# Two-layer vision kernel: the first layer's inverse Fourier product in 64x64 quarters of the array, with accumulators split by parity of the 8x8 block

## What is computed

```python
h = jnp.einsum('oi,bihw->bohw', w_in, x)          # 64 -> 3 x 170 channels
gate, x_sp, x_fr = jnp.split(h, 3, axis=1)
sp = conv_general_dilated(x_sp, w_dw, ... 3x3, feature_group_count=170)
xp = x_fr.reshape(b, 170, H // 8, 8, W // 8, 8).transpose(0, 1, 2, 4, 3, 5)
f = jnp.fft.rfft2(xp) * fft_weight                # over each block of 8x8 pixels
fr = jnp.fft.irfft2(f, s=(8, 8)) ...              # back in place
fused = gelu(gate) * (sp + fr)
return einsum('oi,bihw->bohw', w_out, fused)      # 170 -> 64 channels
```

## Time and profile before

| what | value |
|---|---|
| median of 3 runs | 10511.98 us (10511.55 to 10516.97) |
| the profiled execution: its time, and its span | 10515.79 us, 10514.0 us |
| TensorE clock granted, mean | 0.967 |
| PE busy, share of the span | 9748.7 us, 93% |
| DVE busy | 8528.3 us, 81% |
| ACT busy | 5724.7 us, 54% |
| chain that ended last, PE's share | 81% |

### The profile page before, as it was taken

One profiled execution on the slowest core, in us unless ns is written; L12 is line 12 of the kernel. 1 busy time (PEld: TensorE's weight loads), 2 busy tenths in 40 slices (PEclk: granted clock), 3 DMA queues, 4 the chain that ended last, 5 costly groups with the idle time before them and its releaser, 6 DMA issues.

```text
span 10514.0 us, 163193 instructions
## 1 busy us (share of the span) xinstructions
PE 9748.7 (93%) x60966; PEld 7369.1 (70%) x60966; DVE 8528.3 (81%) x12871; ACT 5724.7 (54%) x9047; POOL 1769.1 (17%) x1824
## 2 busy tenths in 40 slices
PE   1999988999999998998999999899899999989998
PEld 1777765757777775675777777576677777757666
DVE  7788878978788887888878888787886888788787
ACT  0555544656655554454765555455575555445557
POOL 0000003333300001233320000223331000033333
PEclk9999999999999999999999999899999999999999
DMA  4667665475676766446567676635566666564655
GB/s 119 141 139 143 139 144 193 163 225 147 153 147 140 144 140 177 167 169 212 156 149 144 140 143 136 207 142 194 176 172 129 127 128 127 121 210 160 213 155 150
DMA packets 1332286, 1650.52 MB, mean 157 GB/s; under 512 B 843676, under 2 KB 1076524, under 8 KB 1246124
## 3 DMA queue, kind: packets, MB, share of 16 engines
q1 hardware_dynamic: 1331500, 1640.09, 60.7%
HBM read 786.71 MB, written 515.00 MB: 124 GB/s over the span
## 4 chain that ended last, share of the span: by engine, by line
PE 81%; DVE 10%; issue 3%; ACT 3%; DMA 1%; POOL 1%; SPq 1%; DVEq 0%; POOLq 0%; ACTq 0%
PE ps L819 14%; PE ps L1733 12%; PE ps L1746 7%; PE ps L789 6%; PE ps L849 4%; PE ps L1311 4%; PE ps L780 4%; PE ps L833 4%; PE ps L1760 3%; DVE S L1515 3%; PE ps L1304 3%; PE ps L1383 2%; PE ps L873 2%; PE ps L860 2%; PE ps L795 2%
## 5 line engine op out<-in xcount | busy, mean ns | idle before, releaser
L1131 DVE SCALAR_TENSOR_TENSOR F<-U,LW,F 106x512 f32<-106x512 f32 x2048 | 1535.3, 750 | 54.4
L1733 PE MATMUL ps<-fp,Dwr 128*128 128x512 f32 x6144 | 1471.4, 389 | 0.0
L1733 PEld LDWEIGHTS ps<-fp,Dwr 128*128 128x128 f32 x6144 | 1153.3, 188 | 239.5
L1109 DVE TENSOR_TENSOR Z<-ps,LW 128x340 f32<-128x340 f32 x1024 | 522.7, 510 | 822.1 <-PE ps L789 821.1
L943 ACT ACTIVATE XF<-ps 128x340 f32<-128x340 f32 x1024 | 464.5, 454 | 1116.0 <-PE ps L780 1116.0
L819 PE MATMUL ps<-P,WP 128*128 128x512 f32 x3072 | 904.8, 416 | 32.3 <-DMA H<-P 32.3
L1311 PEld LDWEIGHTS ps<-RS,Bc 128*128 128x128 f32 x4096 | 555.0, 200 | 529.3 <-DVE RS L1300 302.3
L819 PE MATMUL ps<-H,WP 128*128 128x512 f32 x3072 | 918.3, 421 | 0.0
L1383 PE MATMUL ps<-fp,Bwr 128*128 128x512 f32 x3072 | 879.4, 426 | 21.3 <-DVE fp L1484 21.3
L1746 PE MATMUL ps<-XP,Cwr 128*128 128x512 f32 x3072 | 824.9, 405 | 75.0 <-DVE XP L1870 75.0
L1311 PE MATMUL ps<-RS,Bc 128*128 128x128 f32 x4096 | 677.1, 295 | 180.8 <-DVE RS L1300 180.8
(11 more groups left out here) (295 smaller groups left out, 20505.0 us busy)
## 6 DMA issues: line engine op xcount, KB each, us to landing
H<-P SPq DMA_DIRECT2D x512, 585.0 KB, 7.2
raw<-x SPq DMA_DIRECT2D x240, 640.0 KB, 11.5
fx_d<-fx SPq DMA_DIRECT2D x112, 1024.0 KB, 3.9
fl_d<-fp SPq DMA_DIRECT2D x112, 1024.0 KB, 5.5
fp<-fl_d SPq DMA_DIRECT2D x112, 1024.0 KB, 5.8
fx<-fx_d SPq DMA_DIRECT2D x112, 1024.0 KB, 5.4
x1h_d<-xo SPq DMA_DIRECT2D x256, 256.0 KB, 9.0
x1v_d<-xo SPq DMA_DIRECT2D x512, 128.0 KB, 7.8
```

The lines of the kernel that those rows point to most:

```text
L1109: e.tensor_tensor(Z[t % 2][:, 2 * c:2 * c + 2, :].rearrange("p a b -> p (a b)"), ps[6][:, 0:2 * HID], Wt, ALU.mult).then_inc(sem["z"], 1)
L1131: ins = e.scalar_tensor_tensor(o, u, wd[0:106, i:i + 1], o, ALU.mult, ALU.add)
L1733: ins = e.matmul(bank(m)[:], Dwr[:, w, c:c + 128], fq[n % 2][x][:, s2, :], start=(s2 == 0 and w == 0 and x == 0), stop=False)
```

## The change

`finv` is called once a tile and makes 32 products in place of 8. Each takes 64 frequencies (the half `hf` = block parity i) and 64 channels (the half q) of a group k, and a new 64x64 constant `Rblk` without zeros, kept beside Rinv in one tile Rall of 192 columns. The four products of a group thus lie in four different quarters of the array, and the two frequency halves write to different banks: the even blocks of the tile to ps2, the odd ones to ps3. So that the convolution and the gate of the same pixels are in the same bank, `conv` and `gate` no longer read 64 neighbouring columns for i, but 8 of every 16 columns (`px8`, and another view of xb). G and the banks are in that order too; `fu` puts the result back in pixel order in F128.

The order changes with it. On TensorE, chunk 0 of `xs` comes where the first `finv` was, and the whole inverse product is ahead of chunk 1 of `xs`. On VectorE both `fu` come after `z` of chunk 0 and three taps.

```diff
-    k["k_Rinv"] = Rb
+    k["k_Rinv"] = np.concatenate([Rb, np.tile(R, (2, 1))], 1)
...
-    Rinv, Rfwd = at("Rinv", [128, 128]), at("Rfwd", [128, 128])
+    Rall, Rfwd = at("Rall", [128, 192]), at("Rfwd", [128, 128])
+    Rinv, Rblk = Rall[:, 0:128], Rall[:, 128:192]
...
-            m = xb[t % 2][:, 512 * i:512 * i + 512].rearrange("p (k r w) -> p r k w", k=4, r=8)
+            m = xb[t % 2][:].rearrange("p (k r b w) -> p b r k w", k=8, r=8, b=2)[:, i]
...
-            col = 64 * i
+
+            def px8(v, r, c):
+                return v[:, r:r + 8, c:c + 128].rearrange("p r (k b w) -> p b r k w", k=8, b=2)[:, i]
+
...
-                    m = (u[:, 0:8, col:col + 64], u[:, 2:10, col + 1:col + 65], v[:, 0:8, col + 2:col + 66],
-                         v[:, 1:9, col:col + 64])[j]
+                    m = (px8(u, 0, 0), px8(u, 2, 1), px8(v, 0, 2), px8(v, 1, 0))[j]
...
-        def finv(t, i):
-            o = ps[2 + i][:].rearrange("p (r c) -> p r c", r=8)
-            for j in range(4):
-                if j % 2 == 0:
-                    e.wait_ge(sem["z"], 4 * (NT * b + t) + 2 * i + j // 2 + 1)
-                ins = e.matmul(o[:, :, 16 * j:16 * j + 16], Z[t % 2][:, 4 * i + j, 0:128], Rinv[:], start=False, stop=(j == 3))
-            ins.then_inc(sem["fi"], 1)
+        def finv(t):
+            for k in range(8):
+                if k % 2 == 0:
+                    e.wait_ge(sem["z"], 4 * (NT * b + t) + k // 2 + 1)
+                for i in range(2):
+                    hf = slice(64 * i, 64 * i + 64)
+                    o = ps[2 + i][:].rearrange("p (r k c) -> p r k c", r=8, k=8)[:, :, k, :]
+                    for q in (slice(0, 64), slice(64, 128)):
+                        ins = e.matmul(o[q], Z[t % 2][hf, k, q], Rblk[hf, :], start=False, stop=(k == 7))
+                    if k == 7:
+                        ins.then_inc(sem["fi"], 1)
...
-            m = F128[s][:].rearrange("c i (a q w) -> c q a i w", q=2, w=64)
+            m = F128[s][:].rearrange("c (a q w) -> c q a w", q=2, w=128)
...
-            finv(t, 0)
             xs(t + 1, 0)
...
                 conv(t, 1, range(3, 5))
+            finv(t)
             xs(t + 1, 1)
-            finv(t, 1)
...
-            e.tensor_tensor(F128[t % 2][:, i, :], ps[2 + i][:], G[t % 2][:, i, :], ALU.mult).then_inc(sem["fu"], 1)
+            o = F128[t % 2][:].rearrange("c (n b w) -> c b n w", b=2, w=8)[:, i]
+            u, v = [x.rearrange("c (n w) -> c n w", w=8) for x in (ps[2 + i][:], G[t % 2][:, i, :])]
+            e.tensor_tensor(o, u, v, ALU.mult).then_inc(sem["fu"], 1)
...
-            fu(t, 0)
             z(t + 1, 0)
             depthwise(t, range(4, 7))
+            fu(t, 0)
             fu(t, 1)
```

More of the change, by code:

```diff
@@ L224, in build @@
     G42 = [at(f"G42{i}", [106, 512]) for i in range(2)]
-    F128 = [at(f"F128{i}", [128, 2, 512]) for i in range(2)]
+    F128 = [at(f"F128{i}", [128, 1024]) for i in range(2)]
     F42 = [at(f"F42{i}", [106, 512]) for i in range(2)]
@@ L718, in ahead_0 @@
         e.dma_start(Rfwd[:], a["k_Rfwd"]).then_inc(sem["rt"], 16)
-        e.dma_start(Rinv[:], a["k_Rinv"]).then_inc(sem["rt"], 16)
+        e.dma_start(Rall[:], a["k_Rinv"]).then_inc(sem["rt"], 16)
     def l0_sp(e, b):
@@ L855, in finv42 @@
                 e.wait_ge(sem["ad"], NT * b + t)
-            R = Rinv[:].rearrange("k (a p c) -> k p a c", a=4, p=2)
+            R = Rinv.rearrange("k (a p c) -> k p a c", a=4, p=2)
             for k in range(8):
```

## The result

The change makes the kernel slower: 10759.5 us (median of 4 runs, 10755.7 to 10764.0) against 10514.5 us for the kernel before beside it (4 runs, 10511.6 to 10517.1). The ratio is 1.0234, with a 95% interval of 1.0221 to 1.0247. That is 245 us, or 0.96 us for each of the 256 tiles. The profiled execution has a span of 10755.5 us. The forecast was 10673 us, 161 us or 0.63 us a tile.

What follows compares the result with a forecast made beforehand. TensorE's queue was taken as the bound. Terms of -0.52, +1.08, +0.05 and +0.02 made +0.63 us a tile, over 256 tiles +161 us on 10512: 10673 us, range 10395 to 10870.

Steps and rivals of the forecast that it cites:

- slower case: Whole kernel: short runs cost as in the sum or some way from it, 10545 to 10870 us, chance 0.46.
- product: Inverse product on TensorE: quarters run four at a time, 1.22 us against 1.74, gaining 0.52 us a tile.
- reads of P and H: Convolution records on TensorE: 56 added runs at 0.8 ns, 45 ns on 24 records, losing 1.08 us a tile.
- reads of xb: Gate and block 4 records on TensorE: runs stay aligned, costing nothing to 0.03 us, 0.02 in the sum.
- `fs` behind the copy: TensorE after chunk 2 of `xs`: `fs` stalls 0 to 0.1 us behind copy XF, taken as 0.05 us lost.
- Rival 2: Inverse product: only two quarters run at a time, 2.08 us, 10600 to 10620 us even with free runs; chance 0.07.
- Rival 3: VectorE becomes the bound if each `fu` grows from 0.68 to over 0.85 us; 10456 us at 0.97; chance 0.03.
- 0.35 us of room: VectorE: z of chunk 1 would be ready 0.35 us before TensorE wants it for `xs` of chunk 2.
- Rival 1: Convolution reads: short runs are free, so the quarters' gain stays, -0.45 us a tile, 10397 us; chance 0.37.
- version with odd columns alone at a cost: Convolution reads: only runs at an odd element cost, 0.4 ns each, adding 0.14 us a tile: 10432 us.

Runs made afterwards that it cites:

- quarters alone: The changed kernel with the convolution's and gate's reads of 64 neighbouring pixels put back, so pixels no longer match: 10413.4 us, ratio 0.9905.
- reads alone: The kernel before with only the new reads in `conv` and the gate, inverse product, order and `fu` unchanged: 10868.9 us, ratio 1.0337.
- the rows of P: The kernel before with four convolution blocks reading P at its 130-element pitch; 64 runs of 8 from column 1 came 68 ns over an aligned read.
- covered kernel: The left-right pairing with chunk 1 of `xs` put ahead of the inverse product, which then lies over the copy XF: 10392.8 us, ratio 0.9884.
- left-right pairing: The changed kernel with groups pairing a left-half and a right-half block, so P and H are read as before: 10417.0 us, ratio 0.9907.
- start 2: The kernel before with a convolution block reading xb in 64 runs of 8 that start two elements behind a 32-byte boundary: 502 ns a record.

## Why the prediction was right, and where it was off

The sign holds, and so does the balance behind it: the quarters gain, the changed reads lose more, and TensorE's queue carries both. What makes a read dear was wrong in it, and that its price came out near was luck, as told below. The measured 10759 us is 86 us above the forecast of 10673, within the slower case's own range. The terms a tile, forecast and found:

| term | forecast | found | from |
|---|---|---|---|
| product | -0.52 | -0.45 to -0.49 | timeline; quarters alone, less the stall |
| reads of P and H | +1.08 | +1.20 | 24 records, 50 ns each |
| reads of xb | +0.02 | +0.15 to 0.2 | reads alone 1.38, less 1.20; the two lines are 48 us busier |
| `fs` behind the copy | +0.05 | +0.095 | with and without cover |
| sum | +0.63 | +0.96 to 1.04 | measured +0.96 |

**The product.** The 64 records take 1.16 us in the timeline after; less the tail of 0.218 that is 0.94 us over 63 steps, 15.0 ns a record or 60 ns a group of four, where 56 were taken from pairs. That they run four at a time is settled, and Rival 2 with its 2.08 us is out. From its start to the next section's start 1.09 us pass (1015.82 to 1016.91), the next section's 0.68 us in place of 0.57 shows the exit of the divided array, and 0.09 us are the entry, as the forecast had them. All in all I count 1.29 us, not 1.22. The deviation is 0.03 to 0.07 us of the 0.52.

**P and H.** The step took 0.8 ns for each added run, from eight runs over 32 aligned ones. The number of runs isn't the quantity: 128 aligned runs are free. It is how many start off a 16-byte piece, by the rule 1.67 ns each. In three of the four blocks that read P and H half of the 64 runs do, 53 ns; before, half or all of eight did, 7 to 13 ns, and P and H lay 7 to 11 ns over L813 in the earlier trace rows. So the price of 0.8 ns for each added run came from fitting rows and for the wrong reason: 56 added runs, half of them off, times 1.67 is 47 ns, and 45 was forecast. In the block from column 1 all of them are off, and the rule has 94 ns there; the rows of P charge only 68 in all for such a read. The medians rose by 58 and 61, and the sums over whole sections, which leave out what the records' tails overlap, by 51 a record. This was named the weakest step; it came close by luck, because half of the added runs happen to be off and the odd column is charged less than its due. Rows of 132 elements would not have rescued it: by the kernel with that pitch two of the four blocks (columns 0) are free and the two others cost 115 and 124 ns, about the same sum. That is worked out, not run.

**xb.** The step said that its runs stay aligned and cost nothing. They stay aligned; but runs of 8 that lie 512 bytes apart were not thought of. They cost 25 to 34 ns in the medians of eight records a tile, and this is the largest miss: 0.13 to 0.18 us of the 0.33 that the forecast lacks; P and H lack 0.12.

**The stall.** The place was right: in every tile the loads of `fs` wait for XF. The cover shows 0.095 us and the timeline 0.08 to 0.09, the upper end of what the step allowed. The busy view hides it, since the waiting shows as a longer record (0.83 us in place of 0.74).

**VectorE.** `fu` with runs of 8 takes what it took, 0.68 us where Rival 3 wanted over 0.85, and in the 320 us above no load of `xs` waits for z, so that rival is out; L1125, ns min/median/max:

```profile
L1125 DVE TENSOR_TENSOR F<-ps,G x512: 678/682/693, 306.7 to 9405.6; 128x512 f32<-128x512 f32 x171
```

The 0.35 us of room that the step found was for z of chunk 1. No run uses it up. What is late in half of the tiles of the covered kernel, whose tile is 0.5 us shorter than before, is z of chunk 0, for which the step worked out no room.

**Rival 1**, that short runs are free, gave 10397 us. It fell for this kernel. Yet its price for a kernel without the reads' cost was good: the quarters alone and the left-right pairing measure 10413 and 10417 us, against 10397 with the stall forecast at 0.05. Its version with odd columns alone at a cost fell with start 2. The 0.4 ns a run of that version was also too low for what it came from: 4 ns between the medians, put down to half of the records of P, is 8 ns for eight runs, 1 ns each.

## What to carry to other kernels

Four quarters of TensorE's array are worth having for products of 64 by 64, but choose the pieces that share a group so that the other operands of the same banks keep their reads; here the left-right pairing, with the product put over a copy, turns +245 us into -122. Before changing the view of a moving operand of 4-byte elements, count the runs that start off a 16-byte boundary, at 1.3 to 1.7 ns each, and not the runs, and expect some 22 to 34 ns a record for runs of 8 that lie 512 bytes apart; a row pitch that is a multiple of four elements makes all rows alike. And when work is taken out from between a producer and its reader, name what covers the copy between them afterwards.

## What the runs showed of the hardware that was not expected

- A moving operand in 128 runs of four elements streams as fast as one in a single run (396 ns both) if each run starts on 16 bytes. Off it, each run costs 1.3 to 1.7 ns from start to start, whatever its length (64 runs: 492 to 506 ns of duration against 397, 324 to 327 ns from start to start against 233).
- Aligned runs of 8 elements read 512 bytes apart cost up to 0.5 ns each over the same ones read 64 bytes apart (431 against 397 ns). Runs of 16 elements read 512 bytes apart are nearly free (392 ns).
- With rows 130 elements apart and an odd start, 68 ns are charged where the rule has 107 (462 ns where it has some 500). This stays open.
- Groups of four products of 64x64 by 64 columns follow one another every 58 to 60 ns from start to start, hardly more than a pair's 56, though each brings four weight loads (L855 as above: 64 records in 1.16 us).
